# Selective scan: every second input product as a matmul with a diagonal of B, and rows of C spread by loads

## The reference, cut to what matters

```
x_dbl = xb @ W_x                       # xb: silu of a convolution, 256 channels
dt_low, Bm, Cm = split(x_dbl, [64, 80])
dt = softplus(dt_low @ W_dt + b_dt)
step:  h = h * exp(A * dt_t) + (x_t * dt_t) * B_t     # for each channel d and state n
       y = sum_n h[d, n] * C_t[n]
out = ((y + D * xb) * silu(z)) @ W_out
```

## Time and profile before

| | busy us | share of the span |
|---|---|---|
| PE | 2592.7 | 83% |
| DVE | 2327.4 | 75% |
| ACT | 1901.9 | 61% |
| POOL | 1453.0 | 47% |
| mean granted TensorE clock | | 0.919 |

### The profile page before, as it was taken

The page is one execution under the profiler, slowest core; times in us unless marked ns, Lnnn a source line. Parts: engine busy times, 40 slices in busy tenths (PEclk is TensorE's granted clock), DMA queues, the critical chain, the costliest instruction groups (busy, mean ns, idle before and its releaser), DMA issues. The chain is left out here.

```text
span 3116.0 us, 43575 instructions
## 1 busy us (share of the span) xinstructions
PE 2592.7 (83%) x15639; PEld 970.1 (31%) x15642; DVE 2327.4 (75%) x2851; ACT 1901.9 (61%) x3284; POOL 1453.0 (47%) x2030
## 2 busy tenths in 40 slices
PE   7799999997469759999999834877777778998777
PEld 3122222222146412222222224622222323443233
DVE  6899999995136469999999661268999996556567
ACT  3599999995024239999999702475555553325444
POOL 4666666650635356666666116615777773000000
PEclk9799999998689869999999957987999999999799
DMA  4111111106322331111111212111000000331000
GB/s 129 42 26 27 27 30 28 27 19 139 46 68 68 86 99 27 27 26 27 26 26 29 90 42 80 57 58 40 7 7 14 7 7 1 94 99 40 1 0 28
DMA packets 171154, 134.05 MB, mean 43 GB/s; under 512 B 67474, under 2 KB 141586, under 8 KB 170682
## 3 DMA queue, kind: packets, MB, share of 16 engines
q1 hardware_dynamic: 133978, 92.04, 11.3%
q0 software_dynamic: 36800, 39.15, 4.5%
q10 hardware_dynamic: 160, 0.07, 0.0%
HBM read 80.80 MB, written 45.93 MB: 41 GB/s over the span
## 5 line engine op out<-in xcount | busy, mean ns | idle before, releaser
L774 DVE TENSOR_REDUCE a_att_mx<-a_att_s 128x2 f32<-128x1024 f32 x960 | 1118.9, 1217 | 90.5 <-PE a_att_s L649 88.3
L753 ACT ACTIVATE a_att_pt<-a_att_st 128x512 f32<-128x512 f32 x2048 | 1085.2, 604 | 73.9 <-PE a_att_st L678 58.6
L678 PE MATMUL a_att_st<-a_qst,a_kst 50*128 50x512 bf16 x2048 | 650.9, 385 | 5.0 <-ACT a_att_pt L753 1.8
L665 PE MATMUL a_att_av<-a_att_pt,a_att_vst 128*32 128x256 f32 (+1 forms) x7168 | 628.9, 423 | 8.3
L649 PE MATMUL a_att_s<-a_kst,a_qst 48*128 48x512 bf16 x2048 | 584.1, 396 | 61.5 <-PEq L312 32.0
L2373 POOL TENSOR_TENSOR g_xn<-m2s_hs,m2s_cb 128x1024 f32<-128x1024 f32 x128 | 300.8, 2355 | 118.9 <-DVE m2s_hs L2340 64.3
L678 PEld LDWEIGHTS a_att_st<-a_qst,a_kst 50*128 50x128 bf16 x2048 | 152.1, 94 | 546.5 <-ACT a_att_pt L753 454.9
L2340 DVE TENSOR_TENSOR_SCAN m2s_hs<-m2s_da,m2s_bps 128x1024 f32<-128x1024 f32 x128 | 292.7, 2287 | 4.4
L665 PEld LDWEIGHTS a_att_av<-a_att_pt,a_att_vst 128*32 128x32 f32 x7168 | 143.1, 108 | 329.0 <-ACT a_att_pt L753 199.0
L530 POOL TENSOR_TENSOR g_area<-g_area 128x512 f32<-128x512 f32 (+3 forms) x256 | 177.9, 695 | 144.0 <-ACT g_area L744 128.9
L2256 PE MATMUL m2s_yps<-g_xn,g_ident 128*128 128x512 f32 x512 | 243.0, 597 | 0.9
(11 more groups left out here) (482 smaller groups left out, 3822.2 us busy)
## 6 DMA issues: line engine op xcount, KB each, us to landing
f_share<-f_comb_rows SPq DMA_DIRECT2D x128, 128.0 KB, 3.0
a_qst<-a_qstk POOLq DMA_DIRECT2D x124, 64.0 KB, 2.3
a_kst<-a_kstk POOLq DMA_DIRECT2D x124, 64.0 KB, 2.4
f_xs<-f_sent SPq DMA_DIRECT2D x20, 396.0 KB, 6.2
a_qstk<-a_qkv_part SPq DMA_DIRECT2D x16, 384.0 KB, 3.6
f_sent<-f0r_zero SPq DMA_DIRECT2D x1, 5148.0 KB, 22.4
a_kstk<-a_qkv_part SPq DMA_DIRECT2D x32, 128.0 KB
a_kstk<-a_qkv_part SPq DMA_DIRECT2D x16, 256.0 KB
```

Of the source, the lines that this page charges most:

```text
L665: mm = pe.matmul(av[32 * gr:32 * gr + 32, at], vst[u][:, kt, h, :], pt[:, 4 * (kt % 4) + 2 * half + h, at], start=kt == 0, stop=kt == 7)
L678: pe.matmul(st[:, e % 3, :], kst[u][64 * h:64 * h + STACK, kt * P:(kt + 1) * P], qst[u][64 * h:64 * h + STACK, half * CH:(half + 1) * CH], ...
L753: act.activation(pt[:, e % 16, :], st[:, e % 3, :], ACT.Exp, scale=scale).then_inc(exp_done, 1)
L774: dve.tensor_reduce(mx[:, par, 2 * cut:2 * cut + 2], s1[:, cut % 2, :, :], AX.X, ALU.max).then_inc(s1_used, 1)
```

## The change

In the odd steps the product dtx * B on DVE goes. With tokens on the partitions, the product is a matmul: for each of the 8 tiles of 128 tokens, the weights are dtx turned (`dtx_t`, tokens x channels), the moving operand is a diagonal matrix `diag` with B of these tokens, and the result, channels x tokens, lands in `bps` as the DVE product would have. PE turns dtx once a segment (8 transposes, in step 12 of the segment before), ACT copies it from PSUM; ACT makes the diagonals, 8 activations per odd step, each the identity times a column of `b_tok`; `b_tok`, B with tokens on the partitions, is made once, from a load of the 16 rows of B, 32 transposes and a copy. Even steps keep their two bf16 matmuls and the product.

C is no longer spread by PE and copied by ACT in any step: the dt stage copies the 32 rows of B and C in f32 (`whole`, one ACT copy more per chunk) and stores them to memory (`bc_dram`); the scan stage loads one row of C per step into all 128 partitions of `cb`, which now has four buffers; the load for step k waits until POOL is through with step k - 4. The first steps' loads wait until B is turned, since its rows lie in `cb` until then. The loads of z move into the same loop on SP.

```diff
@@ mamba_dt_stage: SP, PE, ACT
+                for c in range(NCH):
+                    sp.wait_ge(whole_done, c + 1)
+                    sp.dma_start(bc_dram[:, cols(c)], whole[:, c % 2, :]).then_inc(whole_out[c % 2], 16)
...
+                        pe.wait_ge(whole_done, c - 1)
...
+                    if c >= 2:
+                        act.wait_ge(whole_out[c % 2], 16 * (c // 2))
+                    act.copy(whole[:, c % 2, :], xp[64:96, c % 2, :]).then_inc(whole_done, 1)
                     act.copy(bcs[0:32, cols(c)], xp[64:96, c % 2, :]).then_inc(hi_done, 1)
@@ mamba_scan_stage: SP
+                sp.dma_start(b_rows, bc_dram[0:NS, :]).then_inc(b_here, 16)
                 for weights in ahead:
                     weights.load(sp)
...
+                sp.wait_ge(b_turned, 1)
+                for k in range(STEPS):
+                    q, n = k // NS, k % NS
+                    if n == 6:
+                        if q >= 2:
+                            sp.wait_ge(gated, q - 1)
+                        sp.dma_start(zb[:, q % 2, :], zs[:, q % 2, span(q)]).then_inc(z_in[q % 2], 16)
+                    if k >= RING:
+                        sp.wait_ge(hc_done, k - RING + 1)
+                    sp.dma_start(cb[:, k % RING, :], bc_dram[NS + n:NS + n + 1, span(q)].to_broadcast([P, SEQ])
+                                 ).then_inc(c_in[k % RING], 16)
@@ mamba_scan_stage: PE
+                def turn(q):
+                    pe.wait_ge(dtx_done, q + 1)
+                    if q == 0:
+                        pe.wait_ge(b_copied, 1)
+                    else:
+                        pe.wait_ge(dtx_copied, q)
+                    for j in range(TILES):
+                        mm = pe.transpose(aux[:, j // 4, (j % 4) * P:(j % 4 + 1) * P], dtx[:, q % 2, j * P:(j + 1) * P], g.ident[:, :])
+                    mm.then_inc(dtx_turned, 1)
...
+                pe.wait_ge(b_here, 16)
+                for t in range(NT):
+                    mm = pe.transpose(aux[:, 0, t * NS:(t + 1) * NS], b_rows[:, t * P:(t + 1) * P], g.ident[0:NS, 0:NS])
+                mm.then_inc(b_turned, 1)
...
+                    if by_pe(k):
+                        pe.wait_ge(dtx_copied, q + 1)
+                        pe.wait_ge(diag_done, diags(k) + 1)
+                        for j in range(TILES):
+                            mm = pe.matmul(bps[:, k % 2, j // 4, (j % 4) * P:(j % 4 + 1) * P], dtx_t[:, q % 2, j, :],
+                                           diag[:, diags(k) % 2, j, :], start=True, stop=True)
+                    else:
...
-                    if k >= 1:
-                        pe.wait_ge(c_copied, k)
-                    for f in range(2):
-                        mm = pe.matmul(cps[:, f, :], sel[:, NS + n:NS + n + 1].to_broadcast([96, P]),
-                                       bcs[:, (2 * (q // 2) + f) * CH:(2 * (q // 2) + f + 1) * CH], start=True, stop=True)
-                    mm.then_inc(c_ready, 1)
+                    if k == 0:
+                        turn(0)
+                    if n == 12 and q + 1 < SEGS:
+                        turn(q + 1)
                     if k >= 3:
                         accumulate(k - 3)
@@ mamba_scan_stage: ACT
+                def scale_ident(k):
+                    q, n = k // NS, k % NS
+                    d = diags(k)
+                    if d >= 2:
+                        act.wait_ge(b_ready, k - 3)
+                    for j in range(TILES):
+                        last = act.activation(diag[:, d % 2, j, :], g.ident[:, :], ACT.Copy,
+                                              scale=b_tok[:, q // 2 * TILES + j, n:n + 1])
+                    last.then_inc(diag_done, 1)
...
-                    act.copy(cb[:, k % 2, :], both(cps[:, :, :])).then_inc(c_copied, 1)
+                    if k == 0:
+                        act.wait_ge(b_turned, 1)
+                        act.copy(b_tok[:, :, :].rearrange("p t n -> p (t n)"), aux[:, 0, :]).then_inc(b_copied, 1)
+                        act.wait_ge(b_copied, 1)
+                        take_turned(0)
+                    if n == 13 and q + 1 < SEGS:
+                        take_turned(q + 1)
+                    if k + 1 < STEPS and by_pe(k + 1):
+                        scale_ident(k + 1)
@@ mamba_scan_stage: DVE, POOL
-                    dve.tensor_tensor(over, dtx[:, q % 2, :], over, ALU.mult).then_inc(dbx_done, 1)
-                    dve.wait_ge(dbx_done, k + 1)
+                    if not by_pe(k):
+                        if n == 0:
+                            dve.wait_ge(dtx_done, q + 1)
+                        dve.tensor_tensor(over, dtx[:, q % 2, :], over, ALU.mult).then_inc(dbx_done, 1)
+                        dve.wait_ge(dbx_done, k + 1 - diags(k))
...
-                    pool.wait_ge(c_copied, k + 1)
+                    pool.wait_ge(c_in[k % RING], 16 * (k // RING + 1))
```

More of the change, by code:

```diff
@@ L2085, in _, with mamba_dt_stage @@
                 silu(NCH - 1)
-def mamba_dt_stage(nc, g, name, w, xs, dt, bcs, ahead):
+def mamba_dt_stage(nc, g, name, w, xs, dt, bcs, bc_dram, ahead):
     with Stage(nc, name) as s:
@@ L2096, in mamba_dt_stage @@
         rest, mid = s.sb("rest", [32, CH]), s.sb("mid", [32, CH], BF16)
-        warm = s.sb("warm", [P, 1])
+        warm, whole = s.sb("warm", [P, 1]), s.sb("whole", [32, 2, CH])
         xp, vp = s.ps("xp", [96, 2, CH]), s.ps("vp", [P, 3, 2, CH])
@@ L2102, in mamba_dt_stage @@
              "exp_done", "lost_done", "corr_done", "ln_done", "pool_sum", "dve_sum", "dt_done"))
+        whole_done, whole_out = s.sem("whole_done"), [s.sem(f"whole_out{u}") for u in range(2)]
         corr_a = g.xn[:, :].rearrange("p (c i t) -> p c i t", i=2, t=CH)
@@ L2111, in _ @@
                     weights.load(sp)
+                for c in range(NCH):
+                    sp.wait_ge(whole_done, c + 1)
+                    sp.dma_start(bc_dram[:, cols(c)], whole[:, c % 2, :]).then_inc(whole_out[c % 2], 16)
+                for u in range(2):
+                    sp.wait_ge(whole_out[u], 16 * NCH // 2)
             @block.tensor
@@ L2211, in _, with mamba_scan_stage @@
                 dve.wait_ge(bc_step, 4 * NCH)
-def mamba_scan_stage(nc, g, name, w, xs, dt, bcs, z_dram, ahead):
+def mamba_scan_stage(nc, g, name, w, xs, dt, bcs, bc_dram, z_dram, ahead):
     with Stage(nc, name) as s:
-        NS, SEGS = 16, 2 * BATCH
+        NS, SEGS, RING = 16, 2 * BATCH, 4
         STEPS = SEGS * NS
+        TILES = SEQ // P
         sel = s.sb("sel", [96, 2 * NS], BF16)
@@ L2223, in mamba_scan_stage @@
         aneg = s.sb("aneg", [P, 2, NS])
-        cb = s.sb("cb", [P, 2, SEQ])
+        cb = s.sb("cb", [P, RING, SEQ])
         da, hs = s.sb("da", [P, 4, SEQ]), s.sb("hs", [P, 3, SEQ])
@@ L2236, in mamba_scan_stage @@
         span = lambda q: slice(q // 2 * SEQ, (q // 2 + 1) * SEQ)
-        out_bank = lambda c: cps[:, c % 2, :] if c < 2 or c >= 6 else bps[:, (c - 2) // 2, c % 2, :]
+        by_pe = lambda k: k % 2 == 1
+        diags = lambda k: sum(by_pe(j) for j in range(k))
+        out_bank = lambda c: aux[:, c % 2, :] if c < 2 or c >= 6 else bps[:, (c - 2) // 2, c % 2, :]
         with nc.Block() as block:
@@ L2297, in _, with take_turned @@
             def _(act):
+                def scale_ident(k):
[7 more added lines that the diff above has]
+                    last.then_inc(diag_done, 1)
+                def take_turned(q):
+                    act.wait_ge(dtx_turned, q + 1)
+                    if q >= 2:
+                        act.wait_ge(b_ready, NS * (q - 1))
+                    act.copy(dtx_t[:, q % 2, :, :].rearrange("p j d -> p (j d)"), both(aux[:, :, :])).then_inc(dtx_copied, 1)
                 act.wait_ge(w.here, w.all)
@@ L2358, in weigh_input @@
                 def weigh_input(q):
+                    if q >= 2:
+                        pool.wait_ge(dtx_turned, q - 1)
                     pool.tensor_tensor(dtx[:, q % 2, :], dt[:, q % 2, span(q)], xs[:, q % 2, span(q)],
```

36 lines of the change are left out of this document (17 added, 19 removed).

## The result

Four runs of the changed kernel took 3073.8 to 3080.4 us, median 3077.39; the kernel before, with one more run, 3121.06. The ratio is 0.9857, 95% interval 0.9838 to 0.9877. The profiled execution took 3075.9 us, span 3074.2, 41.8 us less than before.

A forecast was written before the change was run, and what follows sets the result against it. DVE was taken to bound the selective scan. Its term of -75 us, +17.5 for waits on PE, +12.5 for the start and +1.2 for the dt stage gave -44 us: 3076 us, range 3052 to 3110.

The forecast's parts named there:

- DVE's term: Selective scan: every odd step loses its DVE product, a pair falls from 6.89 to 5.70 us, -75 us.
- PE's list: Selective scan: PE's work grows to 5.66 us a pair against DVE's 5.70, plus 0.9 us of turning a segment.
- Rival (a): PE becomes the bound through weight loads that cannot overlap matmuls; a pair takes 7.4 us, 3162 us; chance 0.1.
- The touching of the lists: DVE waits for late PE before step 13's scan (0.8) and the closing operation (1.7); 2.5 us a segment, +17.5 us.
- PE's two stops: PE waits about 1 us at POOL's first late product, and catches up during DVE's 1.2 us closing operation.
- ACT: Selective scan: eight small activations per odd step at 0.31 us each; 4.7 of 5.70 us a pair, costing nothing.
- The loads of C: Scan stage: each step's 512 KB row load lands in 3.8 us with 8.5 us available, so it is hidden.
- The dt stage: One more ACT copy per chunk, 0.58 us, seen only in the first two chunks; +1.2 us (0 to +4.6).
- The start: Scan stage's start: load, turning, copies and activations put the second scan at 2171 to 2173 us, not 2159.5; +12.5 us.
- +9 if they go faster: Lower bound of the scan stage's start cost, +9 us, if the transposes of 16 columns go faster.
- The signs: Scan stage near 405 us, DVE idle some 30 us, PE busy over 90%; wrong if second scan before 2167 or after 2178.

The follow-up runs named there:

- three_quarters: The changed kernel with diagonals in three of four steps instead of every second; 3063.59 us, ratio 0.9928 to the kernel before.
- pool_short: The changed kernel with POOL's gate product and, from the third segment, its dtx product on 32 of 1024 columns; 3032.15 us, ratio 0.9830 to before.
- quarter: The changed kernel with diagonals in every fourth step instead of every second; 3062.06 us, ratio 0.9924 to the kernel before.
- two_sums: The changed kernel with the sum over states in two PSUM buffers and the closing operation one step later; 3028.45 us, ratio 0.9801 to before.
- c_rows_only: The kernel before with only the loads of C's rows added, every product of B still on DVE; 3089.64 us against 3087.79, ratio 1.0003.
- after_again: The changed kernel run again, unchanged, on another chip; 3038.43 us, ratio 0.9834 to the kernel before.
- turn_later: The changed kernel with the turning of dtx one step later, behind the diagonal matmuls of step 13; 3042.73 us, ratio 0.9848 to before.
- late_two_spread: late_start and two_sums together, plus POOL's gate product one step earlier and the turning one step later; 3021.29 us, ratio 0.9784 to before.
- late_start: The changed kernel with the first diagonal in step 7, B and dtx turned beside the first steps; 3032.31 us, ratio 0.9805 to before.
- b_rows_too: late_start with B's rows also loaded where DVE keeps the product, without B matmuls and bf16 splitting; 3069.30 us, ratio 0.9927 to before.

## Why the prediction was right

*DVE's term.* Forecast -75 us at 5.70 us a pair. Measured 5.62 to 5.66, in the mean 5.64: a scan behind a scan follows at 2.20 us, with the full overlap, not at the 2.25 chosen. -79 us for 63 pairs.

*PE's list.* Forecast 1.78 for the diagonals, 5.66 a pair, 0.9 for the turning. Measured 1.79, 5.65, 0.88. Line 367 was the right row, and three_quarters shows the list deciding to 0.2 us a segment. The rule against the change, that loads overlap only with differing row groups (the Trainium skill, "TensorE: Matmul & The Clock Gate", Part 3, "The mechanism"), would have given 3.5 us for the sixteen; the trace has 1.95 from the first start to the last end. So the measurement decides against that rule. The prediction took one sentence of the section; by another sentence of the same section of the Trainium skill, PE pulls a load ahead of matmuls in flight also when it goes to the background weight buffer. The trace agrees with that one. In the 392 us of the scan stage PE is busy 372.5 us and its loading of weights 229.8, so much of the loading lies beside matmuls. Rival (a) is out.

*The touching of the lists.* Forecast 2.5 us a segment, 0.8 and 1.7 at the two places. Measured 0.7 and 1.6, each counted from start to start or as idle time, and 17.3 us in all against 17.5. The places and sizes were right, one cause was not: the wait before the closing operation was put down mainly to POOL's lateness, and pool_short shows 1.5 us of it without. PE's own list, turning included, is enough for it: quarter takes the list down and leaves 0.4 us. PE's two stops were named too: about 1 us at the first late product of POOL, measured 0.7, and 1.2 us behind the closing operation in which PE catches up, measured 1.3. Not seen was that this gap and DVE's wait ahead of it are one meeting, which a second buffer and a later closing operation take away (two_sums).

*ACT.* Forecast 0.31 per small activation, measured (2.44 - 0.39) / 7 = 0.29; hidden, but for the chain at the start.

*The loads of C.* Forecast hidden, 3.8 us; landed in 3.9. c_rows_only puts their price at -2 to +4 us by the interval of its ratio, and at 2.2 us for the first one by its trace.

*The dt stage.* Forecast +1.2, measured -0.4. ACT's third copy was covered from the first chunk on: DVE's first operations had waited 2.5 us for the exponential behind it, and waits 1.7 now.

*The start.* Forecast 12.5, measured 10.8. Two pieces were off and partly cancelled: the load landed 4.3 us after its issue, not 3.4, and the 32 transposes of 16 columns took 3.56 us, half of the 7 worked out from 128-column ones. At a granted 0.50 they follow each other in 0.11 us. The bound "+9 if they go faster" had named it. The diagonal matmuls took 3.65 us, the lower clock's price, where the forecast stood between 1.8 and 3.6.

*The signs.* From its first instruction to the end of the last scan the stage takes 402 us (405 named), DVE is idle 24 of 392 us (30 named), PE is busy 95% of them, and the second scan begins at 2176.7, inside the named 2167 to 2178 even with the 6.7 us from the stages ahead.

*Not foreseen.* The end of the stage, +2.3 us: with the last two scans back to back, POOL has two products with C left where it had one, and PE's last sums wait for the second. In quarter, whose last step keeps its product, the end of the stage is 18.6 us instead of 21.9.

The forecast of 3076 us met 3077.4, and that close a hit is luck. The parts that the change touches erred by -4.2, -1.7, -1.6 and +2.3, together -5: in the traces the two stages are 49 us shorter, not 44. The routing stage, which the change leaves alone, was 6 us longer in the second execution and covered it. Where both kernels ran on one chip (after_again), the change is worth 51 us. What was right for its reasons is the mechanism: DVE's term, PE's list and the size of their coupling.

## What to carry to other kernels

When an operation is taken off the engine that bounds, write the lists of the others for the same period first: the gain ends where the second list is as long, and a full in-order engine turns each further microsecond into a wait (0.88 for 0.88 here). Moving work along a full list gained nothing here (turn_later, late_two_spread); taking away a place where two engines wait for each other in turn did (two_sums), and so did laying a preparation beside steps that don't need it yet (late_start), each worth 8 to 12 us. Before an operand is moved from PSUM to SBUF, look at what the neighbour engine does at that time: in b_rows_too this alone cost 38 us.

## What the runs showed of the hardware

- A matmul of 128 f32 columns with its own weight load costs 0.111 us per instruction in a row of 16, against 0.107 for a quarter of a 512-column one (0.43 from start to start), so the load adds next to nothing; over 1024 instructions the mean recorded duration is 279 ns, the spacing less than half of it. PE stays at a granted 1.00 at 99.9% busy (three_quarters).
- Transposes of 16 columns at a granted clock of 0.50 follow at 0.11 us, half of what was worked out from 128-column ones (0.22).
- A 4 KB row read 128 times from memory lands like a plain 512 KB load, in 3.6 to 4.2 us (medians of the runs), and 159 to 191 GB/s of it beside the scan slow neither DVE (product 1.21 us, scan 2.28 to 2.29) nor POOL (2.36 to 2.37).
- With both operands of a DVE product in SBUF, it and POOL's f32 product don't run side by side: of b_rows_too's 101 lengthened ones, each began while the other engine's was under way and took longer by what was left of that, less 0.14 us (POOL's up to 3.4 instead of 2.4 us, DVE's up to 3.4 instead of 1.2). With one operand in PSUM, both kept their times (1.21 and 2.36).
- The kernel before took 3121 us on one chip and 3088 to 3091 on three others. In the traces of both kernels, the one stage with indirect transfers took 322 and 328 us on the first and 289 to 296 on the others.
